# A fused attention and Mamba kernel whose written-out order of steps, and the banks of its products, are drawn up anew

## The reference

```
# layer 0: attention                     # layer 1: Mamba-2 with a gate on channels
h    = group_norm(x)                     u = layer_norm(x over channels)
q,k,v = h @ qkv_w.T + qkv_b              z, xBC, dt = split(u @ in_w.T)
attn = softmax(q k^T / sqrt(C))          xBC = silu(causal conv over 4 taps)
x    = attn v @ proj_w.T + b + x         state = state * exp(dt A) + dt x B^T
                                         y = state C + D x;  y *= silu(z); rms norm
                                         out = y @ out_w.T
                                         x + out * sigmoid(mlp(mean of out))
```

## Time and profile before

| | us |
|---|---|
| median of 3 runs | 293.25 |
| lowest, highest | 291.04, 295.36 |
| the profiled execution: first to last instruction (span) | 289.1 |
| lowest run less that span | 1.9 |
| median less that span | 4.2 |

### The profile page before, as it was taken

One profiled execution on the slowest core, in us unless ns is written; L12 is line 12 of the kernel. 1 busy time (PEld: TensorE's weight loads), 2 busy tenths in 40 slices (PEclk: granted clock), 3 DMA queues, 4 the chain that ended last, 5 costly groups with the idle time before them and its releaser, 6 DMA issues. The chain is left out here.

```text
span 289.1 us, 6193 instructions
## 1 busy us (share of the span) xinstructions
PE 262.4 (91%) x1992; PEld 224.1 (78%) x1992; DVE 238.4 (82%) x517; ACT 210.1 (73%) x414; POOL 113.3 (39%) x114
## 2 busy tenths in 40 slices
PE   3999999999999999989899997899899996999691
PEld 2889978888887788778888696787898885576581
DVE  5795767447869899899999999989998998797933
ACT  2346678968999758859868974877587967888260
POOL 7000043152055201196454172333751166756171
PEclk9999999999999999999999999999999999999995
DMA  5920000040004400000265000330007100000013
GB/s 160 409 101 2 0 2 1 6 144 0 2 0 130 96 0 2 0 2 1 73 161 140 0 2 0 105 83 2 0 6 194 63 1 2 36 0 3 0 39 146
DMA packets 10987, 15.29 MB, mean 53 GB/s; under 512 B 1515, under 2 KB 5708, under 8 KB 10956
## 3 DMA queue, kind: packets, MB, share of 16 engines
q1 hardware_dynamic: 10412, 14.69, 16.3%
q10 hardware_dynamic: 544, 0.21, 0.3%
HBM read 12.70 MB, written 2.20 MB: 52 GB/s over the span
## 5 line engine op out<-in xcount | busy, mean ns | idle before, releaser
L1157 PEld LDWEIGHTS attn_out<-values,pT 128*128 128x128 f32 x512 | 62.1, 191 | 5.8 <-issue 4.5
L1157 PE MATMUL attn_out<-values,pT 128*128 128x129 f32 x512 | 65.5, 275 | 0.3 <-DVE res L985 0.3
L974 DVE TENSOR_REDUCE neg_max<-scores 128x1 f32<-128x1024 f32 x32 | 39.0, 1219 | 11.9 <-PE scores L1157 11.7
L649 ACT ACTIVATE probs<-scores,neg_max 128x512 f32<-128x512 f32 x64 | 41.6, 684 | 9.1 <-DVE neg_max L974 7.8
L655 ACT ACTIVATE pT<-turn 128x512 f32<-128x512 f32 x64 | 37.5, 594 | 11.3 <-PE turn L1230 11.0
L1230 PE MATMUL turn<-ident,probs 128*128 128x128 f32 x256 | 37.4, 274 | 1.7 <-ACT pT L655 1.7
L575 POOL TENSOR_TENSOR pre<-pre,th 128x512 f32<-128x512 f32 x16 | 22.0, 1373 | 42.6 <-ACT pre L681 39.6
L1230 PEld LDWEIGHTS turn<-ident,probs 128*128 128x128 f32 x256 | 29.9, 142 | 5.6 <-issue 3.5
L561 POOL TENSOR_TENSOR ln_rstd<-ln_var,neg_half 128x4 f32<-128x4 f32 x8 | 11.4, 1430 | 55.7 <-DVE ln_var L996 55.6
L1067 DVE TENSOR_TENSOR_SCAN L<-L,ident 128x512 f32<-128x512 f32 x24 | 28.9, 1219 | 0.7 <-DMA L<-decay_rows_d 0.7
L1157 PE MATMUL scores<-h_hi,q_hi 128*128 128x512 f32 x64 | 28.2, 441 | 0.6 <-DVE q_lo L970 0.6
(11 more groups left out here) (219 smaller groups left out, 606.4 us busy)
## 6 DMA issues: line engine op xcount, KB each, us to landing
L<-decay_rows_d SPq DMA_DIRECT2D x24, 256.0 KB, 3.9
res<-in_x_tok SPq DMA_DIRECT2D x4, 512.0 KB, 8.1
out<-res SPq DMA_DIRECT2D x8, 256.0 KB, 2.1
x_all<-in_x SPq DMA_DIRECT2D x3, 512.0 KB, 8.4
decay_in<-decay_rows_d SPq DMA_DIRECT2D x24, 64.0 KB, 3.6
x_all<-in_x SPq DMA_DIRECT2D x2, 256.0 KB, 3.1
winT<-in_in_wT SPq DMA_DIRECT2D x1, 194.0 KB, 6.9
wqkv<-in_qkv_w ACTq DMA_DIRECT2D x1, 192.0 KB, 4.0
```

What stands on the lines that cost most here:

```text
L649: act.activation(probs[:, i % 2, half_of(h)], scores[:, half_of(h)], ACT.Exp, bias=neg_max[:, i:i + 1]).then_inc(exp_done.sem, 1)
L974: V.tensor_reduce(neg_max[:, n:n + 1], scores[:, :], AX.X, ALU.max, negate=True).then_inc(max_ready.sem, 1)
L1157: return T.matmul(o, w, v, start=start, stop=stop)
```

## The change

Only the table is different. All the lines behind it, and so each step's instructions, its waits and its operands apart from the bank, are the same. Each engine issues as many steps as before. Two lines of the table, of 69, before and after:

```diff
-pT15a wr0a PV13a exp0b exp1b T0b@0 inv6a conv_bc0a wo_s S2b res6a bc0a pT0b conv_bc1a S3b zv0a PV14a bc1a xob1b term2a
-PV15a cd0a bc2a zt0a V0b@1 conv_bc2a inv7a max1b T1b@0 bc3a InX0a@2 res7a conv_bc3a exp2b stats6a stats7a exp3b S4b
...
+stats4a T14a@1 S0b conv_bc0a pT14a S1b stats5a PV12a conv_bc1a PV13a zt0a V0b@1 raw_x0a sp1a max0b exp0b T15a@0 sp2a
+inv6a S2b exp1b S3b pT15a term2a T0b@0 res6a PV14a PV15a max1b sp3a zv0a pT0b exp2b inv7a exp3b v0b T1b@0 S4b pT1b
```

More of the change, by code:

```diff
@@ L78 @@
[L78 to L82, removed]
@@ L103 @@
[L103 to L107, removed]
@@ L128 @@
-hdn0c to_end1d c1d BT1d@2 st0d xend1d SeB0c@1 bt1d tha0c G1d@2 stc0d gated0c gated1c Yo0d@0 m4d U1d@1 yo0d m5d st1d
-yo_dx0d stc1d Y0d@1 m6d Yo1d@0 y0d m7d g0d yo1d Y1d@2 yo_dx1d fin1b sq0d y1d Ss0d@0 g1d store1b Out0d@2 ms0d sq1d
-y_pow0d o_raw0d Ss1d@1 o0d Out1d@0 ms1d y_pow1d Pl0d@2 o_raw1d fin0c o1d Pl1d@0 pl0d fin1c store0c pl1d SeA0d@1 hdn0d
-SeB0d@0 store1c tha0d gated0d gated1d fin0d fin1d store0d store1d
+gn_stats0 warm3 gn_mm10 kq_mm gn_dev0 gn_mm20 gn_ve0 kq_ev vp_mm gn_pow0 gn_aff0 h0a h_hi0a h1a h_lo0a h_hi1a warm5
@@ new lines @@
+dec0c conv_x1c to_end1b xdt1b dA0c cd0c res7c max2d Yo0b@2 stats7c T3d@1 yo0b conv_bc1c ln_ve1c gate1b SeA0a@1 xend1b
+ln_pow1c Y0b@0 hdn0a exp4d term2c yo_dx0b SeB0a@1 tha0a G1b@2 exp5d gated0a y0b S6d g0b m4b PV0d u_tok1c DAT0c@0 S7d
+m5b rows0c wr0c U1b@1 conv_x2c conv_bc2c v1d UT1c@0 PV1d T4d@0 m6b m7b max3d sq0b conv_bc3c u1c bc0c bc1c pT3d pT4d
+inv0d st1b InBC1c@0 th_bc0c Dt1c@2 raw_bc1c res0d T5d@1 Ss0b@0 gated1a bc2c dt_x1c silu0c PV2d sp_exp1c l0c exp6d pT5d
+dd1b exp7d sp9c sp10c T6d@0 fin0a S8d term3c InZ0c@2 conv_x3c sp11c sp12c ms0b sp13c T7d@1 BT0c@1 l1c l2c stc1b pT6d
@@ new lines @@
+sp13d XsT0d@2 sp14d sp15d fin1b raw_x1d raw_bc1d os0c Pl0c@0 sp16d conv_x4d sp17d pl0c xdt0d term3d Cum1d@1 L2d@0
+Ss1c@2 conv_x5d l2d L3d@0 conv_x6d dA1d dec1d cd1d ms1c dA_rows1d DAT1d@1 conv_bc4d conv_x7d l3d dA_T1d y_pow1c th_x1d
+Out1c@2 G0d@0 Dec1d@1 o1c term4d to_end0d xs1d L4d@2 conv_bc5d xend0d m0d m1d conv_bc6d decay1d m2d L5d@1 l4d os1c
+term5d l5d m3d XsT1d@2 L6d@0 xdt1d Pl1c@1 store0b pl1c U0d@2 gate1d conv_bc7d l6d SeA0c@0 th_bc1d hdn0c L7d@1 silu1d
+SeB0c@0 l7d st0d BT1d@1 to_end1d tha0c gated0c stc0d xend1d gated1c bt1d store1b Yo0d@0 yo0d U1d@1 yo_dx0d c1d G1d@2
@@ L132 @@
+Y0d@0 st1d m4d y0d stc1d g0d m5d m6d m7d Yo1d@0 yo1d Y1d@2 yo_dx1d y1d g1d sq0d Ss0d@1 ms0d Out0d@0 sq1d Ss1d@2
+o_raw0d ms1d y_pow0d Out1d@0 Pl0d@1 o0d y_pow1d fin0c o_raw1d store0c fin1c Pl1d@0 pl0d pl1d store1c o1d SeA0d@1 hdn0d
+SeB0d@0 tha0d gated0d gated1d fin0d fin1d store0d store1d
 """.split()
```

106 lines of the change are left out of this document (53 added, 53 removed).

## The result

| | before, beside it | after |
|---|---|---|
| median, us | 293.35 | 277.05 |
| lowest, highest | 291.04, 295.36 | 276.65, 279.15 |
| span of the profiled execution | 289.1 | 274.8 |

I had predicted 291.3, with a range of 284.5 to 298.5.

The account below looks back on a forecast made before the run. PE bounds up to 96.3 us, PE and DVE together to 238.3, then batch 3's chain. Span 289.1 - 4.3 + 2.4 = 287.2; the same -1.9 against 293.25 gives 291.3 us, range 284.5 to 298.5.

Parts of the forecast that it names:

- No order can take out more than 8.6 us: Between first scores and last PV, PE's shown idleness of 8.6 us was taken as the most any order could remove.
- rival B: All PE idleness between first scores and last PV goes, with no payment in the tail: -8.6 us, 284.7; chance 0.17.
- Term 1: Between the attention's row maxima, more evenly spread work shortens the fullest queues from 213.0 to 208.7 us: a gain of 4.3.
- Term 2: Behind the last maximum, work moved there from batch 2 lengthens the tail by 2.4 us, bounds 0 and 3.0.
- Term 3: At batch 3's end, G1d goes behind U1d and st1d ahead of all four multiplications: 0, bounds -0.3 and +1 us.
- Banks and DMAs, costed at nothing: Bank waits were counted within PE's idle 8.6 us, and DVE work was to cover the DMA landings: 0.
- No order wins clock: Over the whole kernel, the clock was already granted in full up to the last slice, so no order gains there.
- The rule against it: DVE instructions block while POOL holds the shared ports: 7.6 us in L869 and L1013, which the order may change.
- rival C: POOL and DVE meetings rise or fall by half, 3.8 us either way: 287.5 to 295.1; small changes counted in the forecast's 0.42.
- A: From batch 2's first maximum on, DVE has more work left: +3.1 us, 296.4, up to 299.4; chance 0.24.
- D: Across the kernel, engines wait for the same producers whatever the order, so no change: 293.25 us; chance 0.17.
- The 4.2 us between span and time: For the whole kernel, the median of runs was put 4.2 us above the profiled span when forecasting the time.

Follow-up runs that it names:

- e1: New order up to the first scores of batch 2 (S0c), the remaining steps in the old sequence; ratio 1.0016 to the kernel before.
- e2: New order up to the first scores of batch 3 (S0d), the remaining steps in the old sequence; ratio 1.0023 to the kernel before.
- e13: The changed kernel with G1d alone put back ahead of Yo0d; ratio 0.9633 to the kernel before.
- e14: The kernel before with only the 29 steps from st0d to y1d in the new sequence; ratio 1.0105 to the kernel before.
- e3: The kernel before with 54 of POOL's arithmetic instructions replaced by three fills each of the same tile; ratio 0.9661 to the kernel before.
- e5: New order up to the last PV (PV15d), the rest in the old sequence; ratio 0.9646 to the kernel before.
- e9: The kernel before with each product moved to the bank whose reader stands earliest in the table; ratio 1.008 to the kernel before.
- e11: The changed kernel with the old table's banks, as far as possible, and its old sequence of DMA issues; ratio 0.9819 to the kernel before.
- e16: New order up to the last PV (PV15d), the rest in the old sequence, the same kernel as e5 measured again; ratio 0.9698 to the kernel before.
- e7: The changed kernel with the old table's banks where the order allows, 106 of 218 products changed; ratio 0.9838 to the kernel before.
- e8: The changed kernel with SyncE's DMA issues in the old table's sequence; ratio 0.9615 to the kernel before.

## Why the prediction was wrong, step by step

**"No order can take out more than 8.6 us": this step failed, and with it rival B's price and the lower end of the range.** I read the idle time of the earlier trace rows as all of PE's waiting. Counted by starts, PE waited 19.1 us in that stretch, and 10.2 of it went. The busy time of the earlier trace rows was no floor: 262.4 fell to 255.9 with the same products. The evidence was in the trace before: a sum of start-to-start distances would have given it. The sign that I had named came true, shown idleness fell to 3.4 us where I had said near 4, and it says little about the gain.

**Term 1, evenness, -4.3: right in kind, too small.** Between the maxima 12.9 us went. With fills on POOL in both orders, 7.5 of it remain, so 5.4 are meetings and 7.5 what the order does for PE's waits otherwise. I predicted 4.3 for that by a count that had met the trace before; it charged mean durations with the meetings in them, and knew nothing of pauses. The count of 208.7 us was no lower bound: 199.6 were measured. The longest time between maxima fell to 13.5 us, as forecast. That evenness is the cause of these 7.5 us is only argued: no run changed it alone, and e1 and e2 show no gain from the front part of the table.

**Term 2, the tail, +2.4: wrong sign.** The time behind the last maximum fell by 1.9. There is more work in it, as said (1.4 us of PE behind `PV15d`), but PE waits 4.5 us less there.

**Term 3, 0: too small, and outside its bounds of -0.3 and +1.** The stretch from the transposes of B to `Yo1d` is 1.3 us shorter. How much of that is the sequence's own is open: e13 undoes one of its moves only and leaves `c1d` late, which costs 3.3 to 4.3 us, and e14, with this sequence in the old order, is slower by 3.1 us. I had priced the products (1.13 us) and not what they wait for in a queue with no other work.

**Banks and DMAs, costed at nothing: right in the sum, wrong as a reason.** I said that a bank's waits are part of the 8.6 us. They are worth 10.5 us if they do not fit, the issues 4.0. Both tables have fitting ones, which is why the sum did not suffer; that was luck, since I had not looked at it.

**"No order wins clock": right for these two traces, wrong as a rule.** Both are at full clock up to the last slices, but the traces of e1, e3, e5 to e9 and e11 to e14 lose it in between, mostly behind pauses of PE of 1.6 to 2.4 us.

**The rule against it, and rival C: right mechanism, price too small, and in the good direction.** I looked at two lines, 7.6 us, and allowed for half of that. All of DVE's instructions together spent 38.4 us above their minimum, 12.3 of which went. That gave about 7 us of time (4 to 10) where 3.8 was my bound.

**A** (a backlog on DVE) is out: DVE is full from `S0d` to the last `PV` (0.8 us idle), but the stretch holds more work of both engines than before and PE waits in it for 3.1 us instead of 9.4. **D** is out by the ratio.

**The 4.2 us between span and time** were no fixed addition: in each run with both on record the time stands 1.7 to 2.2 us above its own span. The 4.2 set a median against the span of an execution quicker than the median. The forecast of a difference does not suffer from it.

The account: of 15.3 us, some 7 are meetings of POOL and DVE, some 8 are fewer waits of PE, of which the sequence around and behind the last `PV` (e16) may hold up to 5 to 6; these overlap and do not add exactly, and a share for each place in the middle remains open. No kernel of the experiments that keeps all the arithmetic beat the changed one.

## What to carry to other kernels

Where PE is "busy" for over 90%, sum the distances from start to start and compare them with the usual one of each kind before you call the idle time a bound; do the same with the durations of DVE's instructions, which held its waits for POOL here. An order, its banks and its DMA sequence are one design: a part of it moved alone, however sensible, was worth nothing or cost 1 to 10 us here. And price a pause of PE of about 2 us at up to twice its length if work follows: behind about half of such pauses the clock fell here.

## What the runs showed of the hardware

- **TensorE's clock often halves behind a short pause, but not by rule.** Behind pauses of 2.31 us (e7), 2.04 (e8) and 1.66 (e13) the granted clock was 0.68, 0.61 and 0.67 in the next four or five us, the lower level (1.2 GHz) for most of them, and in e7 products of 512 columns started 0.43 us apart instead of 0.23. Over all 18 traces, between 18 us and 15 us before the end, PE has 32 pauses of 1.57 to 2.35 us; behind 15 the clock fell, at the latest 1.8 us after the pause's end, and behind 17 it did not. Two further falls have no such pause ahead of them (e7 at 268.6, e9 at 258.9). The same pause goes either way: e5 and e16 are one kernel, and behind 2.35 us before `Yo1c` the clock fell in e5 and behind 2.34 it stayed at 1.00 in e16. The changed kernel has 1.82 us before `Cum1b` at 143.20 and kept 1.00, e13 with 1.83 us at the same place fell to 0.57 in the four us from 144; the kernel before has 1.67 us before `Cum0d` at 241.05 and kept 1.00, and e14, with the same steps up to there and the same pause, fell to 0.64 in the four us from 244.
- **Most of the spread between executions goes with the clock.** Over the 64 executions of the kernel before that ran beside the experiments, span and mean clock go together (correlation -0.92): 288.2 to 290.1 us at a mean clock of 0.992 to 0.994, and 293.1 to 293.7 at 0.971. Where in these executions the clock fell is not on record.
- **DVE's waits for POOL are large and look like work.** Replacing POOL's arithmetic by fills about as long took 17.0 of the 38.4 us that DVE spends above the shortest of each kind, and 9.9 us off the time. What the other 21.4 us are, equal in both orders, is not shown.
